# A fused attention and feed-forward kernel on one Trainium2 core: the second attention's output projection as three fp16 passes, with a new step list and new banks

## The chip, the cores and the metric

The kernel runs on one core of one Trainium2 chip. The engines spoken of are TensorE (PE, with PEld for its weight loads), VectorE (DVE), ScalarE (ACT), GpSimd (POOL) and SyncE (SP, which issues the DMAs). The metric is the device time in microseconds (us) of the core; lower is better.

## The reference

For x of 4 x 2048 x 512 in float32, the result of four residual stages:

```
x = x + attn_a(layernorm(x))     # linear attention, 16 heads of 64, prefix sums over tokens
x = x + ffn(layernorm(x))        # int8-rounded matmul with rhs (512 x 512)
x = x + attn_b(layernorm(x))     # gated, decaying state, 16 heads of rank 16
x = x + ffn(layernorm(x))
```

The change lies in the end of `attn_b`, where a state M per head is carried over the tokens:

```
M = M * decay + einsum('bhr,bhd->bhrd', g_t * k_t * scale, v_t)
y = einsum('bhr,bhrd->bhd', q_t, M)
...
out = Y @ out_w.T + out_b
hres = x + out
return (hres - mu) / sqrt(var + 1e-05) * ln_g + ln_b
```

## The kernel before, in words

The 8192 tokens are cut into 64 chunks of 128. For each chunk the work is some 110 named steps; a step belongs to one engine. The table `ORDER` lists every step with a lag. Time is a row of slots; in slot s a step of lag l works on chunk s - l, and each engine walks its own steps in the order of the table. So in one slot PE works on the first attention's projections of chunk s (lag 0), its scores of chunk s - 1, and the second attention of chunk s - 3. Ten slots are written out, then a loop of two slots an iteration runs up to slot 63, then four slots (64 to 67) drain the pipe, each with fewer steps.

Each engine stays in order, so a step that waits holds everything behind it on its engine. `BANK` gives each matmul result one of the 8 PSUM banks; `c.take(unit)` waits until the bank's former user has been read out, `c.read` until it is full, `c.done` until it has been read. `COUNTS` only lists the semaphore values that the loop keeps in registers.

The steps around the change, with their names:
- `yb` (PE) ends y of a chunk in two banks. `y_e` (ACT) copies both to `yT`, which lies in the tile `turn_q`, with the feature in the partition.
- `out` (PE, `out_`) multiplies `yT` by `wout`, both float32: four matmuls of 128x128 by 128x512, each of which the trace shows as two records.
- `out_e` (DVE) adds the bank to `xnb`; `no_st`, `no_rs`, `no_ap`, `no_f` are the layer norm behind it. `nb_ap` (DVE) then writes the next chunk's normalised input into the same `xnb`; `xTb_h`, `xTb_l`, `xTb_t` (ACT, DVE, SP) split it in fp16 halves and transpose them by DMA; `kb`, `gb`, `qb`, `vb` (PE) are its projections.
- All other projections go through `three_pass`: high and low fp16 halves of both operands, three matmuls for one. Their weights are split in the set-up, one after the other, each after its largest absolute value has been found (DVE), spread over the partitions (POOL, `partition_all_reduce`) and turned into a power of two (four small DVE instructions).
- `mm0`, `mm1` (PE) are the two feed-forward matmuls, `mm0_e`, `mm1_e` (DVE) read them out, `mm0_a`, `mm1_a` (POOL) add the residual. `s0`, `so0`, `o0`, `u0` and their twins are the first attention's scores, state products and state update; `qk0` to `qk3` its q and k projections, read out by `qk0_e` to `qk3_e` (DVE).

Of the kernel before, what the change touches and what calls it, by code (L numbers as in the profile page):

```python
# [62 lines left out]
BANK = {"v0": 7, "v1": 1, "qk0": 2, "qk1": 4, "qk2": 6, "qk3": 1, "kt0": 6, "s0a": 2, "s0b": 3, "o0a": 4, "o0b": 5,  # L63
        "u0": 0, "kt1": 0, "s1a": 3, "s1b": 0, "o1a": 6, "o1b": 7, "u1": 1, "wo": 0, "mm0": 0, "qb": 2, "kb": 6,
        "vb": 4, "gb": 7, "qr": 5, "kr": 3, "sb0": 6, "sb1": 7, "sb2": 0, "sb3": 1, "y0": 3, "y1": 5, "ub": 1,
        "out": 7, "mm1": 2}
# [117 lines left out]
def hybrid_kernel(nc, x, Wq, Wk, Wv, Wo, bo, q_w, k_w, v_w, Wqr, Wkr, g_w, g_b, logits, out_w, out_b, ln_g, ln_b,  # L184
                  rhs, tables, keeps, out):
    ctx = ExitStack()
    with ctx:
# [1131 lines left out]
```

## Time and profile before

| | us |
|---|---|
| median of 3 runs | 3245.57 (3244.02 to 3248.7) |
| the profiled execution's own time | 3244.64 |
| its span in the trace | 3242.9 |
| PE busy | 3108.5 (96%) |
| DVE busy | 2179.4 (67%) |
| POOL busy | 1016.1 (31%) |
| ACT busy | 564.6 (17%) |

Busy times are unions over an engine's instructions. A matmul's record is longer than its share of the engine, since the next one starts before it ends; the distance from start to start tells what a matmul costs. L numbers are lines of the kernel before, and a helper's line stands for all its callers: L598 to L600 are the three lines of `three_pass`.

### The profile page before, as it was taken

The numbers are of one execution on the slowest core, as the hardware profiler recorded it, in microseconds if no ns is written. First come the engines' busy times: TensorE is split into PE (matmuls) and PEld (weight loads), VectorE is DVE, ScalarE is ACT, GpSimd is POOL, SyncE is SP. The second block draws the span as 40 slices with busy tenths as digits, with TensorE's granted clock in tenths as the row PEclk, the third lists the DMA queues.
The fourth block names the chain that finished last, engine by engine and source line by source line (L and its number), as shares of the span: only waits on it lengthen the run. The fifth ranks groups of instructions, "written<-read, shape, count | busy, mean of one in ns | idle before, by whom it ended". The sixth has DMA issues, their size and how long they took to land.

```text
span 3242.9 us, 104237 instructions
## 1 busy us (share of the span) xinstructions
PE 3108.5 (96%) x44242; PEld 2368.6 (73%) x44242; DVE 2179.4 (67%) x4675; ACT 564.6 (17%) x1048; POOL 1016.1 (31%) x1371
## 2 busy tenths in 40 slices
PE   1599999999999999999999999999999999999995
PEld 1577777777777777777777777777777777777774
DVE  7566766666766666666676676676676666666664
ACT  2111111111111111111111111111111111111111
POOL 0023333333333333333333333333333333333333
PEclk8799999999999999999999999999999999999998
DMA  4122222222222222222222222222222222222221
GB/s 164 50 43 46 40 47 44 40 47 44 40 47 44 47 42 46 46 43 46 46 40 46 46 40 47 44 40 47 44 40 47 44 45 44 44 46 44 46 39 26
DMA packets 383786, 151.88 MB, mean 47 GB/s; under 512 B 353312, under 2 KB 361632, under 8 KB 383392
## 3 DMA queue, kind: packets, MB, share of 16 engines
q1 hardware_dynamic: 383392, 145.56, 24.3%
q8 instruction: 378, 6.19, 0.8%
q14 instruction: 16, 0.13, 0.0%
HBM read 44.83 MB, written 16.78 MB: 19 GB/s over the span
## 4 chain that ended last, share of the span: by engine, by line
PE 95%; DVE 3%; DMA 1%; issue 1%; ACT 0%; POOL 0%; POOLq 0%; SPq 0%; DVEq 0%; ACTq 0%
PE bank L598 20%; PE bank L600 20%; PE bank L599 20%; PE bank L835 7%; PE bank L659 4%; PE bank L685 4%; PE bank L725 3%; PE bank L565 2%; PE bank L789 2%; PE bank L672 2%; PE bank L768 2%; PE bank L699 2%; PE bank L759 2%; PE bank L812 2%; PE bank L799 1%; DVE absmax L1016 1%
## 5 line engine op out<-in xcount | busy, mean ns | idle before, releaser
L598 PE MATMUL bank<-xaT,wq_hi 128*128 128x128 f16 x2048 | 358.6, 220 | 25.7 <-DMA xaT<-xa_split 25.7
L599 PE MATMUL bank<-xaT,wq_hi 128*128 128x128 f16 x2048 | 357.3, 219 | 0.0
L600 PE MATMUL bank<-xaT,wq_lo 128*128 128x128 f16 x2048 | 357.3, 219 | 0.0
L598 PE MATMUL bank<-xaT,wk_hi 128*128 128x128 f16 x2048 | 356.8, 219 | 0.0
L599 PE MATMUL bank<-xaT,wk_hi 128*128 128x128 f16 x2048 | 356.8, 219 | 0.0
L600 PE MATMUL bank<-xaT,wk_lo 128*128 128x128 f16 x2048 | 356.7, 219 | 0.0
L1105 DVE TENSOR_SCALAR work<-bank,eps_q 128x256 f32<-128x256 f32 x256 | 123.4, 482 | 330.4 <-PE bank L600 330.3
L553 POOL TENSOR_TENSOR xf<-xwb,xf 128x512 f32<-128x512 f32 x64 | 81.8, 1277 | 656.7 <-DVE xf L1185 656.7
L598 PEld LDWEIGHTS bank<-xaT,wq_hi 128*128 128x128 f16 x2048 | 200.6, 98 | 56.3 <-issue 48.6
L835 PE MATMUL bank<-wout,turn_q 128*128 128x512 f32 x512 | 233.8, 599 | 1.9 <-ACT turn_q L942 1.9
L530 POOL TENSOR_TENSOR turn_q<-turn_q,cross_q 128x512 f32<-128x512 f32 x64 | 104.5, 1632 | 334.5 <-DVE cross_q L1209 334.5
L599 PEld LDWEIGHTS bank<-xaT,wq_hi 128*128 128x128 f16 x2048 | 200.8, 98 | 8.3
L600 PEld LDWEIGHTS bank<-xaT,wq_lo 128*128 128x128 f16 x2048 | 200.8, 98 | 0.0
L598 PEld LDWEIGHTS bank<-xaT,wk_hi 128*128 128x128 f16 x2048 | 200.7, 98 | 0.0
L599 PEld LDWEIGHTS bank<-xaT,wk_hi 128*128 128x128 f16 x2048 | 200.6, 98 | 0.0
L600 PEld LDWEIGHTS bank<-xaT,wk_lo 128*128 128x128 f16 x2048 | 200.6, 98 | 0.0
L598 PE MATMUL bank<-wv_hi,xaT 128*128 128x512 f16 x512 | 194.0, 379 | 0.0
L599 PE MATMUL bank<-wv_lo,xaT 128*128 128x512 f16 x512 | 194.0, 379 | 0.0
L600 PE MATMUL bank<-wv_hi,xaT 128*128 128x512 f16 x512 | 194.0, 379 | 0.0
L598 PE MATMUL bank<-wo_hi,work 128*128 128x512 f16 x512 | 194.0, 379 | 0.0
L599 PE MATMUL bank<-wo_lo,work 128*128 128x512 f16 x512 | 194.0, 379 | 0.0
L600 PE MATMUL bank<-wo_hi,work 128*128 128x512 f16 x512 | 194.0, 379 | 0.0
(203 smaller groups left out, 8220.6 us busy)
## 6 DMA issues: line engine op xcount, KB each, us to landing
xin<-in_L_attn_a_x SPq DMA_DIRECT2D x64, 256.0 KB, 2.6
out<-xf SPq DMA_DIRECT2D x64, 256.0 KB, 2.1
table<-in_tables SPq DMA_DIRECT2D x64, 192.5 KB, 2.9
work<-in_L_attn_a_Wq SPq DMA_DIRECT2D x1, 2048.0 KB, 7.8
work<-in_L_attn_a_Wk SPq DMA_DIRECT2D x1, 2048.0 KB, 14.0
work<-in_L_attn_a_Wv SPq DMA_DIRECT2D x1, 2048.0 KB, 7.5
work<-in_L_attn_a_Wo SPq DMA_DIRECT2D x1, 2048.0 KB, 8.4
work<-work SPq DMA_TRANSPOSE x128, 3.6
```

The lines of the kernel that those rows point to most:

```text
L530: pool.tensor_tensor(to[:, :, :, :], to[:, :, :, :], cross[:, :, ::-1, :], ALU.add)\
L553: pool.tensor_tensor(xf1[:, c.par, :], xwb[:, c.par, :], xf1[:, c.par, :], ALU.add)\
L565: last = nc.tensor.transpose(bank[:, i * P:(i + 1) * P], src(i), id_)
L598: nc.tensor.matmul(o, a[0], b[0], start=first, stop=False)
L599: nc.tensor.matmul(o, a[0], b[1], start=False, stop=False)
L600: return nc.tensor.matmul(o, a[1], b[0], start=False, stop=last)
L659: last = nc.tensor.matmul(bank[:, tile(i)], qk[h, 1, 4 * g + i, :], qk[h, 0, 4 * g + i, :], start=True, stop=True)
L672: nc.tensor.matmul(bank[t, i * VA:(i + 1) * VA], qk[h, 0, 4 * g + i, t], state_a[h, 4 * g + i, :], start=i == 0, stop=False, skip_group_ch ...
L685: last = nc.tensor.matmul(bank[t, i * VA:(i + 1) * VA], sc[g][:, p, i, t], va[:, 2 * (4 * g + i) + p, :], start=False, stop=i == 3, skip_g ...
L725: last = nc.tensor.matmul(bank[:, :], xqT[w][:, k, :], rhs_q[:, k, :], start=k == 0, stop=k == KD - 1)
L835: last = nc.tensor.matmul(bank[:, :], yT[:, k, :], wout[:, k, :], start=k == 0, stop=k == KD - 1)
L1105: last = nc.vector.tensor_scalar(qk[:, n, m, :].rearrange("p m t -> p (m t)"), bank[:, 256 * n:256 * n + 256], 0.0, e_[:, :], ALU.max, ALU ...
```

## The change

`wout` becomes a pair of fp16 tiles, scaled by a power of two like the other weights, so the set-up finds a ninth maximum. In each chunk y gets its own scale: `y_m` (DVE) takes the largest absolute value of each partition's row of `yT`, `y_r` (POOL) spreads the largest of all partitions, `y_s` (DVE) makes a power of two and its inverse in four instructions on 128x1, `y_h` (ACT) writes the high half and `y_l` (DVE) the low half into `y_split`, which lies in `cross_q`. `out` is twelve fp16 matmuls, and `out_e` multiplies by the inverse scale as it adds. `ORDER`, `BANK` and `COUNTS` are new throughout; the largest lag stays 4. Of the tables two lines are shown.

```diff
-ORDER = [("nf1_st", 4), ("xTb_h", 3), ("wo1", 2), ("xTb_l", 3), ("qk3", 1), ("s0", 1), ("wo_e", 2), ("kt0", 1),
+         ("y_e", 3), ("y_m", 3), ("aT1_h", 1), ("u1", 1), ("s0", 0), ("aT1_l", 1), ("qk2", 0), ("mm0", 2),
+         ("aT0_t", 1), ("mm1_a", 4), ("ub_e", 3), ("y_r", 3), ("y_s", 3), ("y_h", 3), ("u1_e", 1), ("mm0_e", 2),
+         ("wo0", 1), ("y_l", 3), ("st_o", 4), ("mm0_a", 2), ("qk2_e", 0), ("out", 3), ("nb_st", 2),
...
-        wout = sb("wout", [P, KD, D])
+        wout = (sb("wout_hi", [P, KD, D], F16), sb("wout_lo", [P, KD, D], F16))
...
+        y_split = cross_q[:, :, :, :].rearrange("p j e t -> p (j e t)").bitcast(F16)\
+            .rearrange("p (s k t) -> p s k t", s=2, k=KD)
...
-            for slot in range(8):
+            for slot in range(9):
                 pool.wait_ge(wmax, slot + 1)
...
+            def y_r(c):
+                c.wait(y_reduced, c.count())
+                pool.sem_inc(y_reducing, 1)
+                pool.partition_all_reduce(y_all[:, :], y_max[:, :], P, ABSMAX).then_inc(y_known, 1)
...
             def out_(c):
                 bank, f = c.take("out")
-                c.done("y0")
-                c.done("y1")
+                c.wait(y_halved, c.count())
                 for k in range(KD):
-                    last = nc.tensor.matmul(bank[:, :], yT[:, k, :], wout[:, k, :], start=k == 0, stop=k == KD - 1)
+                    last = three_pass(bank[:, :], (y_split[:, 0, k, :], y_split[:, 1, k, :]), w_part(wout, k, slice(0, D)),
+                                      k == 0, k == KD - 1)
...
+            def y_h(c):
+                c.wait(y_scaled, c.count())
+                c.filled("sb3")
+                nc.scalar.activation(y_split[:, 0, :, :], yT, ACT.Copy, scale=y_scale[:, :]).then_inc(y_hi, 1)
...
-                        if name == "out":
-                            nc.vector.tensor_copy(wout[:, k, :], bank[:, :]).then_inc(e, 1)
-                        else:
...
+            def y_m(c):
+                c.done("y0")
+                c.done("y1")
+                nc.vector.tensor_reduce(y_max[:, :], yT.rearrange("p k t -> p (k t)"), AX_X, ALU.max,
+                                        apply_absolute_value=True).then_inc(y_reduced, 1)
+
+            def y_s(c):
+                c.wait(y_known, c.count())
+                nc.vector.tensor_scalar(y_small[:, :], y_all[:, :], 2.0 ** -80, 2.0 ** -12, ALU.max, ALU.mult)\
+                    .then_inc(y_bounded, 1)
+                c.wait(y_bounded, c.count())
+                nc.vector.tensor_scalar(y_exponent[:, :].bitcast(U32), y_small[:, :].bitcast(U32), 0x7F800000, None,
+                                        ALU.bitwise_and).then_inc(y_power, 1)
+                c.wait(y_power, c.count())
+                nc.vector.tensor_scalar(y_scale[:, :].bitcast(U32), y_exponent[:, :].bitcast(U32), 0x7F800000, None,
+                                        ALU.bitwise_xor).then_inc(y_scaled, 1)
+                nc.vector.tensor_scalar(y_unscale[:, c.par:c.par + 1], y_exponent[:, :], unscale[:, SOUT:SOUT + 1], 0.5,
+                                        ALU.mult, ALU.mult)
+
+            def y_l(c):
+                c.wait(y_scaled, c.count())
+                c.wait(y_hi, c.count())
+                nc.vector.scalar_tensor_tensor(y_split[:, 1, :, :], yT, y_scale[:, :], y_split[:, 0, :, :], ALU.mult,
+                                               ALU.subtract).then_inc(y_halved, 1)
+
             def out_e(c):
                 bank, e = c.read("out")
                 c.wait(xn_bias, c.count())
-                nc.vector.tensor_tensor(xnb[:, :], bank[:, :], xnb[:, :], ALU.add).then_inc(e, 1)
+                nc.vector.scalar_tensor_tensor(xnb[:, :], bank[:, :], y_unscale[:, c.par:c.par + 1], xnb[:, :],
+                                               ALU.mult, ALU.add).then_inc(e, 1)
```

The new list in words, for PE within one slot: `v0 v1 s1 so0 so1 u0 o0 o1 kb gb qb kt1 kr vb kT qr mm1 qk0 sb ys qk1 ub yb u1 s0 qk2 mm0 wo0 out wo1 kt0 qk3`. Before it was: `wo1 qk3 s0 kt0 v0 kt1 v1 kb gb qb s1 so0 so1 o0 u1 u0 o1 kr vb kT qr qk0 sb ys qk1 mm1 mm0 ub yb qk2 out wo0`. `s0`, `kt0` and `qk3` have lag 0 now where they had lag 1.

PE before, in the loop, from the end of `qk2` (the last fp16 rows with `wk`) through `out` (`wout`, four matmuls) to the start of `wo0`:

```order
L598 MATMUL bank<-xaT,wk_hi 128x128
L599 MATMUL bank<-xaT,wk_hi 128x128
L600 MATMUL bank<-xaT,wk_lo 128x128
L123 REGISTER_ALU
L835 MATMUL bank<-wout,turn_q 128x512 x4
L123 REGISTER_ALU
L598 MATMUL bank<-wo_hi,work 128x512
```

PE in the changed kernel, at the end of `wo0` (`wo`) and the start of `out` (`wout`), outside the loop, where the same steps follow each other:

```order
L618 MATMUL bank<-wo_hi,work 128x512
L619 MATMUL bank<-wo_lo,work 128x512
L620 MATMUL bank<-wo_hi,work 128x512
L618 MATMUL bank<-wout_hi,cross_q 128x512
L619 MATMUL bank<-wout_lo,cross_q 128x512
L620 MATMUL bank<-wout_hi,cross_q 128x512
```

`out` stands behind the twelve matmuls of `wo0` now instead of ahead of them, and is made of the same form.

PE in the changed kernel's loop, from `ub` (L845) and `yb` (L832) on, through `u1` (L719) and `s0` (L679) into `qk2`:

```order
L845 MATMUL bank<-vbs,turn_k 32x64 x8
L121 REGISTER_ALU
L832 MATMUL bank<-work,vbs 32x128 x16
L719 MATMUL bank<-va,work 64x65 x8
L679 MATMUL bank<-work 128x128 x8
L618 MATMUL bank<-xaT,wq_hi 128x128
```

`u1` and `s0` have moved between `yb` and `qk2`; behind `qk2` come `mm0`, `wo0` and then `out`.

DVE before, in the loop, from `ub_e` (u_tmp) over `qk1_e`, `qk2_e` and `nb_st` to `out_e` (L1248):

```order
L1242 TENSOR_TENSOR u_tmp<-bank,own_head 128x128
L123 REGISTER_ALU
L1105 TENSOR_SCALAR work<-bank,eps_q 128x256
L1105 TENSOR_SCALAR work<-bank,eps_k 128x256
L1105 TENSOR_SCALAR work<-bank,eps_q 128x256
L1105 TENSOR_SCALAR work<-bank,eps_k 128x256
L1070 BN_STATS stats_b<-xwb 128x6
L1072 COPY carrier<-eps 128x1
L1073 BN_AGGR mean_var_b<-stats_b 128x2
L123 REGISTER_ALU
L1248 TENSOR_TENSOR xnb<-bank,xnb 128x512
```

DVE in the changed kernel's loop, from `y_m` (L1270) over `aT1_l`, `ub_e`, the four instructions of `y_s`, `u1_e` and `mm0_e` (L1207) to `y_l` (L1290):

```order
L1270 TENSOR_REDUCE y_max<-turn_q 128x1
L1115 TENSOR_TENSOR work<-work 128x512
L121 REGISTER_ALU
L1264 TENSOR_TENSOR u_tmp<-bank,own_head 128x128
L1276 TENSOR_SCALAR y_small<-y_all 128x1
L1279 TENSOR_SCALAR y_exponent<-y_small 128x1
L1282 TENSOR_SCALAR y_scale<-y_exponent 128x1
L1284 TENSOR_SCALAR y_unscale<-y_exponent,unscale 128x1
L1161 SCALAR_TENSOR_TENSOR state_a<-state_a,keep_a,bank 128x260
L121 REGISTER_ALU
L1207 SCALAR_TENSOR_TENSOR xf<-bank,row_scale,rs_row 128x512
L1290 SCALAR_TENSOR_TENSOR cross_q<-turn_q,y_scale,cross_q 128x512
```

Six new instructions stand on DVE between `yb` and `out`, and the last of them is queued behind `mm0_e`, which waits for `mm0`.

## Rows read from the trace of the kernel before

**Rows 1.** The page's first part: busy us, share of the span, instructions.

```profile
PE 3108.5 (96%) x44242; PEld 2368.6 (73%) x44242; DVE 2179.4 (67%) x4675; ACT 564.6 (17%) x1048; POOL 1016.1 (31%) x1371
```

**Rows 2.** Stretch from the first to the last full slot: length, busy per engine, clock, DMA.

```profile
117.60:3098.00 2980.40, 2978.94 (x42812) 2273.25 (x42813) 2015.06 (x4368) 519.48 (x985) 959.01 (x1279) 1.00 0.25 44
```

**Rows 3.** Chain that ended last: start us, us, what; two neighbouring slots.

```profile
1573.75 3.49 PE bank L835 x8
1621.90 3.49 PE bank L835 x8
```

**Rows 4.** Timeline of PE, qk2, out, wo: start us, us, engine, line, operation.

```profile
1522.74 0.23 PE L598 MATMUL bank<-xaT,wq_hi 128*128 128x128 f16 x1
...
1525.43 3.65 PE L835 MATMUL bank<-wout,turn_q 128*128 128x512 f32 x8
1528.92 0.38 PE L598 MATMUL bank<-wo_hi,work 128*128 128x512 f16 x1
...
1534.10 0.22 PE L598 MATMUL bank<-xaT,wq_hi 128*128 128x128 f16 x1
```

**Rows 5.** Groups by line: xcount, busy us, mean ns, idle before and its releaser.

```profile
L659 PE MATMUL bank<-work 64*128 64x128 f32 x2048 | 148.7, 285 | 0.0
L1171 DVE TENSOR_REDUCE amax<-xf 128x1 f32<-128x512 f32 x128 | 84.9, 664 | 0.1
L699 PE MATMUL bank<-va,work 128*64 128x65 f32 x2048 | 70.6, 222 | 0.0
L1093 DVE TENSOR_TENSOR cross_k<-xnb,cross_k 128x512 f16<-128x512 f32 x64 | 44.0, 688 | 5.4 <-ACT cross_k L918 0.7
L878 ACT ACTIVATE xa_split<-xna 128x512 f16<-128x512 f32 x64 | 40.3, 630 | 143.2 <-DVE xna L1078 92.1 <-PE bank L600 51.1
```

**Rows 6.** Timeline of all engines around both feed-forward matmuls of one slot.

```profile
1615.99 1.89 PE L725 MATMUL bank<-rhs_q,xqT 128*128 128x512 bf16 x8
1617.05 1.61 DVE L1185 SCALAR_TENSOR_TENSOR xf<-bank,row_scale,rs_row 128x512 f32<-128x512 f32 x2 [1.70 <-PE bank L725]
1617.81 0.43 PE L825 MATMUL bank<-vbs,turn_k 128*32 128x64 f32 x16
1617.88 1.28 POOL L553 TENSOR_TENSOR xf<-xwb,xf 128x512 f32<-128x512 f32 x1 [10.50 <-DVE xf L1185]
```

**Rows 7.** Timelines of POOL and of DVE where two large instructions meet.

```profile
1644.79 1.27 POOL L530 TENSOR_TENSOR turn_k<-turn_k,cross_k 128x512 f32<-128x512 f32 x1 [4.68 <-DVE cross_k L1209]
...
1645.02 1.59 DVE L1093 TENSOR_TENSOR xa_split<-xna,xa_split 128x512 f16<-128x512 f32 x1
```

**Rows 8.** Timelines of DVE, ACT and PE in the set-up, weights bv and out.

```profile
77.28 2.28 DVE L1016 TENSOR_REDUCE absmax<-work 128x1 f32<-128x2048 f32 x1
80.04 0.15 DVE L1019 TENSOR_SCALAR absall<-absall 128x1 f32<-128x1 f32 x1 [0.48 <-POOL absall L490]
...
80.61 2.42 ACT L862 ACTIVATE wbv_hi<-bank,scale 128x512 f16<-128x512 f32 x4 [4.42 <-DVE scale L1022]
...
84.13 1.21 DVE L1016 TENSOR_REDUCE absmax<-work 128x1 f32<-128x1024 f32 x1
...
89.72 3.67 PE L565 MATMUL bank<-ident,work 128*128 128x128 f32 x16 [6.77 <-DMA work<-in_L_attn_b_out_w]
...
94.34 3.62 DVE L1034 TENSOR_REDUCE xwa<-work 128x512 f32<-128x2048 f32 x1
```

**Rows 9.** Timeline of PE in the drain, from slot 65 into slot 66.

```profile
3187.68 1.08 PE L812 MATMUL bank<-work,vbs 128*32 128x128 f32 x32
3189.41 3.67 PE L835 MATMUL bank<-wout,turn_q 128*128 128x512 f32 x8 [0.64 <-ACT turn_q L942]
3202.18 0.26 PE L598 MATMUL bank<-xbT,wbk_hi 128*128 128x128 f16 x1 [9.11 <-DMA xbT<-cross_k]
```

**Rows 10.** Timelines of DVE and PE at the first chunk's first projection.

```profile
115.31 0.69 DVE L1093 TENSOR_TENSOR xa_split<-xna,xa_split 128x512 f16<-128x512 f32 x1 [0.78 <-ACT xa_split L878]
...
119.06 0.27 PE L598 MATMUL bank<-xaT,wq_hi 128*128 128x128 f16 x1 [25.66 <-DMA xaT<-xa_split]
```

More of the change, by code:

```diff
@@ L60 @@
 MAX_LAG = max(LAG.values())
[L63 to L66, printed above, removed]
+BANK = {"v0": 6, "v1": 7, "qk0": 4, "qk1": 3, "qk2": 6, "qk3": 5, "kt0": 7, "s0a": 0, "s0b": 1, "o0a": 2, "o0b": 3,
+        "u0": 7, "kt1": 7, "s1a": 4, "s1b": 0, "o1a": 1, "o1b": 5, "u1": 5, "wo": 4, "mm0": 7, "qb": 4, "kb": 6,
+        "vb": 0, "gb": 0, "qr": 2, "kr": 6, "sb0": 0, "sb1": 1, "sb2": 5, "sb3": 2, "y0": 6, "y1": 7, "ub": 4,
+        "out": 5, "mm1": 3}
 BANKS = 8
@@ L201, in hybrid_kernel @@
         rankk = sb("rankk", [P, 2, 2, P])
-        scale = sb("scale", [P, 8])
-        unscale = sb("unscale", [P, 8])
-        SQ, SK, SV, SO, SBQ, SBK, SBV, SBG = range(8)
+        scale = sb("scale", [P, 9])
+        unscale = sb("unscale", [P, 9])
+        SQ, SK, SV, SO, SBQ, SBK, SBV, SBG, SOUT = range(9)
         eps_q = sb("eps_q", [P, 1])
@@ L295, in hybrid_kernel @@
         squares_i = sb("squares_i", [P, 8, 2])
-        absmax = sb("absmax", [P, 8])
-        absall = sb("absall", [P, 8])
-        exponent = sb("exponent", [P, 8])
+        absmax = sb("absmax", [P, 9])
+        absall = sb("absall", [P, 9])
+        exponent = sb("exponent", [P, 9])
         marks = sb("marks", [P, 16])
+        y_max = sb("y_max", [P, 1])
+        y_all = sb("y_all", [P, 1])
+        y_small = sb("y_small", [P, 1])
+        y_exponent = sb("y_exponent", [P, 1])
+        y_scale = sb("y_scale", [P, 1])
+        y_unscale = sb("y_unscale", [P, 2])
         ps = [ctx.enter_context(nc.psum_tensor(f"bank{i}", [P, 512], F32)) for i in range(BANKS)]
@@ L331, in hybrid_kernel @@
         xn_bias = sem("xn_plus_bias")
+        y_reduced = sem("y_max_of_rows")
+        y_reducing = sem("y_max_begun")
+        y_known = sem("y_max_of_all")
+        y_bounded = sem("y_max_bounded")
+        y_power = sem("y_exponent_ready")
+        y_scaled = sem("y_scale_ready")
+        y_hi = sem("y_hi_done")
+        y_halved = sem("y_split")
         b_added = sem("state_b_added")
@@ L377, in hybrid_kernel @@
         NAT = [("q", Wq, SQ), ("k", Wk, SK), ("v", Wv, SV), ("o", Wo, SO)]
-        TRN = [("bq", q_w, SBQ), ("bk", k_w, SBK), ("bv", v_w, SBV), ("g", g_w, SBG), ("out", out_w, None)]
+        TRN = [("bq", q_w, SBQ), ("bk", k_w, SBK), ("bv", v_w, SBV), ("g", g_w, SBG), ("out", out_w, SOUT)]
         parts = {"q": wa["q"], "k": wa["k"], "v": wa["v"], "o": wo, "bq": wb["q"], "bk": wb["k"], "bv": wb["v"],
-                 "g": wg}
+                 "g": wg, "out": wout}
         TASKS = NAT + TRN + [("rhs", rhs, None)]
@@ L558, in _ @@
                            qb_a=turn("q", turn_q, cross_q), kb_a=turn("k", turn_k, cross_k), gb_k=gb_k, ub_a=ub_a,
-                           mm1_a=mm1_a))
+                           mm1_a=mm1_a, y_r=y_r))
         @block.tensor
@@ L864, in _ @@
                         u += 1
-            act.wait_ge(w_hi, 4 + 4 * KD)
+            act.wait_ge(w_hi, 4 + 5 * KD)
             nc.scalar.activation(amax[:, 0:1], ident[:, 0:1], ACT.Copy).then_inc(ready["act"], 1)
@@ L1045, in _ @@
                         dve.wait_ge(f, u_ // BANKS + 1)
-                        if name == "out":
-                            nc.vector.tensor_copy(wout[:, k, :], bank[:, :]).then_inc(e, 1)
-                        else:
-                            hi += 1
-                            dve.wait_ge(w_hi, hi)
-                            w_hi_, w_lo = parts[name]
-                            nc.vector.scalar_tensor_tensor(w_lo[:, k, :], bank[:, 0:src.shape[0]], scale[:, one],
-                                                           w_hi_[:, k, :], ALU.mult, ALU.subtract).then_inc(e, 1)
+                        hi += 1
+                        dve.wait_ge(w_hi, hi)
+                        w_hi_, w_lo = parts[name]
+                        nc.vector.scalar_tensor_tensor(w_lo[:, k, :], bank[:, 0:src.shape[0]], scale[:, one],
+                                                       w_hi_[:, k, :], ALU.mult, ALU.subtract).then_inc(e, 1)
                         u_ += 1
@@ L1272, in _ @@
                           qb_e=turn_parts("q", turn_q, cross_q), kb_e=turn_parts("k", turn_k, cross_k),
-                          gb_e=gb_e, qr_e=qr_e, kr_e=kr_e, sb_e0=sb_e(0), sb_e1=sb_e(1), ub_e=ub_e, out_e=out_e,
+                          gb_e=gb_e, qr_e=qr_e, kr_e=kr_e, sb_e0=sb_e(0), sb_e1=sb_e(1), ub_e=ub_e, y_m=y_m, y_s=y_s,
+                          y_l=y_l, out_e=out_e,
                           no_st=no_st, no_ap=no_ap, no_f=no_f, nf1_st=nf1_st, nf1_ap=nf1_ap, nf1_q=to_int(1),
```

16 lines of the change are left out of this document (9 added, 7 removed), and 48 rows, old and new, of tables (COUNTS, ORDER).

## The prediction

> **What bounds the kernel now.** I read the busy shares first: PE is busy 96% of the span, DVE 67%, POOL 31%, ACT 17% [rows 1]. Then one window from the first full slot to the last: of 2980.4 us PE is busy 2978.9 at the full clock of 2.4 GHz (granted share 1.00), DVE 2015 [rows 2]. So between set-up and drain PE never stands still, and whatever shortens PE's own stream shortens the kernel one for one, as long as nobody makes PE wait. The chain of waits says the same: it consists of PE, and `out` comes back in it every 1621.90 - 1573.75 = 48.15 us, one slot [rows 3]. Sixty-four chunks make 64 x 48.15 = 3082 of the 3242.9 us; the other 161 are set-up (PE's first projection starts at 119.06 [rows 10]), waits in the drain, and its cold clock.
>
> **The projection itself.** Before, `out` starts at 1525.43 and `wo0` behind it at 1528.92: 3.49 us for four float32 matmuls of 512 columns. `wo0` and `wo1` are 24 fp16 matmuls of the very form that `out` gets, and take 1534.10 - 1528.92 = 5.18 us, 0.216 each [rows 4]. Twelve cost 2.59. That is 0.90 us a chunk less, 64 x 0.90 = 57.6 us.
> PE's other work is the same instructions in another order. By the PE timeline a change from fp16 to float32 steps costs up to 0.09 us at the seam. Before, a slot has five such seams that cost something, now four; I take -0.05 us a slot (between 0 and -0.1), -3.2 us.
>
> **Does PE still find everything ready?** The new work in a slot is a chain between `yb` and `out`: `y_e`, `y_m`, `y_r`, `y_s`, `y_h`, `y_l`. None of these ran in the loop before, so I price each by its nearest row. `y_m` is a maximum over 512 columns, 0.66 (L1171) [rows 5]. `y_r` cost DVE 0.48 of idle time in the set-up (`absall` waiting for POOL), and from there to the start of the ACT instruction that needs the scale is 80.61 - 80.04 = 0.57, which is `y_s` up to its third instruction [rows 8]. `y_h` is L878, 0.63; `y_l` is L1093 on `cross_k`, 0.69 [rows 5]. Sum 3.03, with four hand-overs of some 0.1 us: 3.4 us. `y_e` was there before: where nothing else lay between, `out` started 1.73 us after `yb` did [rows 9]. So the halves are ready 5.1 us after the start of `yb`.
> Behind `yb` (1.08 [rows 9]) PE now has `u1` (70.6 / 128 = 0.55), `s0` (148.7 / 128 = 1.16) [rows 5], `qk2` (1525.43 - 1522.74 = 2.69), `mm0` (half of 1617.81 - 1615.99, 0.91 [rows 6]) and `wo0` (2.59 [rows 4]), so it comes to `out` after 9.0 us. The chain by itself has 3.9 us to spare.
> But `y_l` is queued behind `mm0_e` on DVE. `mm0` ends 6.4 us after the start of `yb`; DVE starts to read a feed-forward bank about 0.2 us after its four matmuls (1617.05 against 1615.99 + 0.86, as `mm1` is half of the eight) and takes 0.7 to 0.8 [rows 6]. So `y_l` starts at 7.3 and ends at 8.0, 0.9 us ahead of `out`. Cover for that is `wo0`; without it `out` would wait 1.7 us a slot.
> The other close places I found by laying PE's new list out in time with the old distances: `s0` needs `qk1_e` (about 0.7 to spare), `qk2` needs the bank of `y0` (0.9), `u0` needs `v0_e` (0.9), `o1` needs `s1_e` (1.1), `yb` needs the four masks of `sb` (0.9). None is negative. DVE gets 0.66 + 0.6 + 0.69, about 2 us, more a slot, and was busy for 68% of it [rows 2]; ACT 0.63, POOL 0.36. No engine but PE becomes full. I count zero a slot; the bounds are 0 and 0.4 (below).
>
> A rule speaks against `y_l`. In the trace `xa_split`, which has two inputs in SBUF as `y_l` has, took 1.59 us where POOL's addition of 1.27 had begun 0.23 before it, while the same form took 0.69 on `cross_k` [rows 5, 7]: it ended 0.55 after POOL's. The Trainium skill, page "SBUF — State Buffer", section "SBUF: two separate sides", says why: VectorE and GpSimd share a port pair as an exclusive lock, the first to start keeps it, the other is blocked fully; by that rule, the trace agrees. Now `mm0_a` on POOL and `y_l` on DVE are both let go by `mm0_e`. In the trace POOL starts 0.83 us after DVE's read-out began [rows 6], and DVE's next instruction after 0.7 to 0.75, so `y_l` should win by about 0.1. If it loses, it ends 0.83 + 1.24 + 0.55 = 2.6 us after the start of `mm0_e`, where PE comes to `out` after 2.59 - 0.2 = 2.4; with the hand-over that is up to 0.4 us of waiting a slot.
>
> **Set-up.** `out`'s weights land at 89.7 (PE begins to transpose them), and the next weight maximum could start there. One weight from its maximum to the next one's start is 84.13 - 77.28 = 6.85 us, so DVE would be free for `rhs` at 96.6 instead of 94.34 [rows 8]: +2.2 us (0 to 3).
>
> **Filling the pipe.** Slots 0 to 2 lack the lag-3 steps, so PE comes early. `s0` with lag 0 stands right behind `qk1` and waits for `qk1_e`, some 1.0 us in slot 0, 0.5 in slots 1 and 2. `qk0` of slots 1 and 2 now comes about 10.3 us into its slot; its transposed input needs `s1_e` first (7.7 us into the slot), then the low half and the DMA, 119.06 - 115.31 = 3.75 [rows 10]: 11.4, so 1.1 us twice. Together +4.2 (0 to 8). Before, PE went through here without a wait.
>
> **Draining it.** In slots 64, 65 and 66 the fillers of lag 0 and 1 are gone, so the 3.4 us of the y chain lie open; and there each chunk's `kb` waits for the `out` of the chunk before, since both use `xnb`: 3202.18 - 3189.41 = 12.8 us from one to the other, 9.11 of it idle [rows 9]. In slot 64 `wo0` and `mm0` still fill, but this only moves work ahead of the same chain. So three chunks pay in full: 3 x 3.4 = +10.2 us (7 to 13).
>
> **Sum.** -57.6 - 3.2 + 2.2 + 4.2 + 10.2 = -44.2. The profiled execution took 3244.64 by its own time, 1.74 around its span; it becomes 3200.4. It was 0.9 under the median of the runs, so I forecast 3201 us for the median.
>
> **Rivals.**
> - Dense, and the ends for free: filling and draining hidden by something I overlook, set-up too. 3201 - 16.6 = 3184. For it: DVE is idle for a third of each slot. Against it: the drain is a pure chain, its waits stand in the trace.
> - Thin margins tear: `y_l` loses the port to `mm0_a`, or `s0` or `u0` find their reader late, 0.4 us in each of some 60 slots: +24, 3225. For it: a margin of 0.1 us in the port race, margins under 1 us elsewhere. Against it: the old list has waits as close and shows none.
> - The other side: `y_r` is dear inside the loop. It is the only kind of instruction that POOL had in the set-up alone, and POOL's spans are rough. The chain has 3.3 us to spare until `out` (2.4 until `mm0_e` ends, 0.9 behind it), and the gain is 44 / 60 = 0.7 a slot; so the kernel gets slower once `y_r` costs over 4.0 us more than its 0.48. At 6 us it would be 3201 + 60 x 2.2 + 3 x 5.5 = 3350. For it: a call of 128x512 is longer than one of 128x1 and the loop has other POOL work around it. Against it: eight calls in the set-up, and DVE's wait confirms the 0.48 from outside.
> - Three passes come out still cheaper. The trace has 0.216 us for each of the 512-column fp16 matmuls, in a dense stream with all its weight loads [rows 4]. If such a stream could go at 0.13, `out` would take 1.6 and 64 x 1.0 more would be gained: about 3137. The Trainium skill, page "TensorE: Matmul & The Clock Gate", section "Back-to-back issue gap", gives about 131 ns as the sustained distance at 512 columns; the trace contradicts it.
>
> **How the numbers follow.** Dense slots with ends that cost something 0.66, ends for free 0.12, thin margins 0.13, dear `y_r` 0.07, cheaper passes 0.01, anything else 0.01. The time is that of the first, 3201. Its own range is 3193 to 3210 (set-up, filling, draining and seams at their bounds). The range to hold the time 8 times in 10 reaches to the second and third: 3182 to 3230. A measurement of this kernel tells 0.2% (6.5 us) from no change. The first three cases and the fifth are all faster by more than that: 0.91. Within 0.2% only by a stall that happens to be 0.7 us a slot: 0.02. Slower: 0.07.
>
> **What would show it.** Right: a slot of 47.2 us in the chain; PE busy without a gap from the first full slot to the last; twelve records of 0.38 us in `out`, 0.216 apart; PE idle ahead of `out` only in slots 64 to 66, some 3 to 4 us released by DVE's `y_l`; POOL's reduction near 0.36; `y_l` near 0.7. Wrong: PE idle ahead of `out` in the loop, with `y_l` at 1.3 or more (the port), or with POOL's reduction as releaser; PE idle ahead of `s0`, `u0`, `o1` or `qk2` in each slot; a slot that isn't 0.9 us shorter although PE never waits.

## The result, and the profile after

The changed kernel takes 3525.43 us (median of 4 runs, 3519.92 to 3529.04) against 3245.68 of the kernel before in the same comparison: a ratio of 1.0861, 95% interval 1.0843 to 1.0878. It is slower by 280 us where 44 us of gain were forecast. The profiled execution took 3523.69, its span is 3521.9.

The page's first part, as in [rows 1]:

```profile
PE 3120.6 (89%) x44370; PEld 2358.5 (67%) x44498; DVE 2264.2 (64%) x5064; ACT 612.5 (17%) x1116; POOL 1052.2 (30%) x1436
```

One window inside the run of full slots (columns as in [rows 2]):

```profile
237.00:3400.00 3163.00, 2934.63 (x42050) 2216.80 (x42171) 2072.44 (x4688) 555.33 (x1036) 997.53 (x1340) 0.98 0.21 41
```

PE, busy throughout before, is idle for 228 of these 3163 us, and its granted clock is no longer full. From `out` to `out` a slot now takes 51.95 us in the mean (52 slots) instead of 48.15. The groups by line name the wait (xcount, busy us, mean ns, then the idle time before them and its releaser):

```profile
L569 POOL PARTITION_ALL_REDUCE y_all<-y_max x64 | 26.2, 409 | 870.5 <-issue 870.5
L618 PE MATMUL bank<-wout_hi,cross_q 128*128 128x512 f16 x256 | 115.0, 449 | 170.6 <-DVE cross_q L1290 170.6
L1092 DVE BATCH_NORM_STATS2 stats_b<-xwb 128x6 f32<-128x512 f32 x64 | 44.5, 695 | 325.4 <-POOL xwb L531 325.4
L1276 DVE TENSOR_SCALAR y_small<-y_all 128x1 f32<-128x1 f32 x64 | 9.8, 154 | 373.7 <-POOL y_all L569 373.7
L531 POOL TENSOR_TENSOR xwb<-xwa,xf 128x512 f32<-128x512 f32 x64 | 80.4, 1256 | 456.2 <-issue 442.4
```

The reduction itself takes 0.41 us, as hoped. But before it GpSimd is idle for 870.5 / 64 = 13.6 us by "issue", that is, by nothing the profile shows (part of it GpSimd would be idle anyway, until `y_m` is done), and its next ordinary instruction, the addition of `mm0_a`, waits another 442.4 / 63 = 7.0. DVE's `y_s` loses 5.8 us a slot to the first, `nb_st` 5.1 to the second.

The list of one line's instructions says what stands there. `y_r` (L569) and the helper of GpSimd's additions (L531):

```profile
L569 POOLq MODIFY_POOL_CONFIG  x128: 11/11/11, 231.4 to 3490.2; - x128
L569 POOL PARTITION_ALL_REDUCE y_all<-y_max x64: 408/409/412, 237.4 to 3496.1; - x64
```

```profile
L531 POOLq MODIFY_POOL_CONFIG  x126: 82/83/83, 237.8 to 3451.4; - x126
```

(The three numbers are the least, median and largest duration in ns, then come the first and the last start in us.) Two reconfigurations go ahead of each of the 64 reductions, and two at `mm0_a` behind 63 of them. From the reconfiguration to the reduction it is 237.4 - 231.4 = 6.0 us in the first chunk and 3496.1 - 3490.2 = 5.9 in the last. I call what happens in this time a load of code; the trace shows only the idle time behind the reconfiguration. In the kernel before there was a pair for the reductions too, once:

```profile
L490 POOLq MODIFY_POOL_CONFIG  x2: 11/11/11, 3.6 to 3.6; - x2
```

The first of its eight reductions began at 13.4 us, after a wait for the maximum of the first weights, so the load that goes with it lay under that wait.

One slot in time. DVE and then GpSimd (start us, us, instruction, idle before it and releaser):

```profile
1526.63 0.69 DVE L1270 TENSOR_REDUCE y_max<-turn_q 128x1 f32<-128x512 f32 x1 [0.86 <-ACT turn_q L962]
...
1534.02 0.15 DVE L1276 TENSOR_SCALAR y_small<-y_all 128x1 f32<-128x1 f32 x1 [5.90 <-POOL y_all L569]
...
1534.98 0.74 DVE L1207 SCALAR_TENSOR_TENSOR xf<-bank,row_scale,rs_row 128x512 f32<-128x512 f32 x1
1535.64 0.74 DVE L1290 SCALAR_TENSOR_TENSOR cross_q<-turn_q,y_scale,cross_q 128x512 f16<-128x512 f32 x1
...
1542.21 0.69 DVE L1092 BATCH_NORM_STATS2 stats_b<-xwb 128x6 f32<-128x512 f32 x1 [5.05 <-POOL xwb L531]
...
1543.10 0.72 DVE L1296 SCALAR_TENSOR_TENSOR xnb<-bank,y_unscale,xnb 128x512 f32<-128x512 f32 x1
```

```profile
1533.58 0.41 POOL L569 PARTITION_ALL_REDUCE y_all<-y_max  x1 [13.75 <-issue]
1540.93 1.25 POOL L531 TENSOR_TENSOR xwb<-xwa,xf 128x512 f32<-128x512 f32 x1 [6.95 <-issue]
```

The chain of waits crosses the same place (start us, us, what):

```profile
1527.78 5.80 issue
1533.58 0.42 POOL y_all L569
```

`y_m` is done at 1527.3. Some 0.4 us go to handing over and to the reconfigurations, the wait by "issue" behind them takes 5.80, and at 1533.58 the reduction begins. Then the ordinary code comes back, 6.95 us, with `mm0_a` behind it, `nb_st` behind that on DVE, and `out_e` behind `nb_st`.

PE in the same slot:

```profile
1533.66 0.38 PE L620 MATMUL bank<-wo_hi,work 128*128 128x512 f16 x1
1536.53 0.38 PE L618 MATMUL bank<-wout_hi,cross_q 128*128 128x512 f16 x1 [2.49 <-DVE cross_q L1290]
...
1537.61 0.63 PE L620 MATMUL bank<-wout_hi,cross_q 128*128 128x512 f16 x1
...
1540.59 0.59 PE L618 MATMUL bank<-wo_hi,work 128*128 128x512 f16 x1
```

`out` waits 2.49 us. Its matmuls start 0.216 apart at first and 0.43 apart from 1537.61, so PE has fallen from 2.4 to 1.2 GHz behind the idle time: the twelve take 4.06 us instead of 2.59. The granted clock of the stretch from 1537.90 to 1541.00 is 0.50:

```profile
1537.90:1541.00 3.10, 3.10 (x8) 1.06 (x7) 0.00 (x0) 0.00 (x0) 0.07 (x1) 0.50 0.00 0
```

This happens in 20 of the 52 slots, not in each. In the other 32 `out` takes its 2.59 us, and `qk3` waits 1.7 us for `out_e` instead, since `out_e` now frees `out`'s bank late (63.1 us in 43 slots, the whole run taken together). The two kinds of slot are equally long, 51.8 and 52.0 us: what ends a slot is `out_e`, at the end of GpSimd's way back.

### The profile page after: what moved, and what is told of

Same layout as the page of the kernel before. It is cut to its first block, busy times and chain, and to the rows that moved or that the text cites. A ratio compares the mean times of both kernels' runs of the same rounds, so it can differ in the third digit from the quotient of the medians.

```text
span 3521.9 us, 104781 instructions
## 1 busy us (share of the span) xinstructions
PE 3120.6 (89%) x44370; PEld 2358.5 (67%) x44498; DVE 2264.2 (64%) x5064; ACT 612.5 (17%) x1116; POOL 1052.2 (30%) x1436
## 3 DMA queue, kind: packets, MB, share of 16 engines
q8 instruction: 379, 6.21, 0.7%
## 4 chain that ended last, share of the span: by engine, by line
PE 65%; issue 21%; DVE 8%; POOL 3%; ACT 1%; DMA 1%; POOLq 0%; ACTq 0%; DVEq 0%; SPq 0%
PE bank L618 16%; PE bank L620 15%; PE bank L619 15%; PE bank L705 3%; PE bank L679 2%; PE bank L809 2%; PE bank L692 2%; POOL xwb L531 2%; PE bank L788 2%; PE bank L779 2%; PE bank L745 1%; PE bank L585 1%; PE bank L832 1%; DVE y_max L1270 1%; PE bank L719 1%
## 5 line engine op out<-in xcount | busy, mean ns | idle before, releaser
L618 PE MATMUL bank<-xaT,wq_hi 128*128 128x128 f16 x2048 | 361.6, 221 | 94.9 <-DVE xnb L1296 63.1
L618 PE MATMUL bank<-xaT,wk_hi 128*128 128x128 f16 x2048 | 361.3, 221 | 0.0
L619 PE MATMUL bank<-xaT,wk_hi 128*128 128x128 f16 x2048 | 361.1, 221 | 0.0
L569 POOL PARTITION_ALL_REDUCE y_all<-y_max x64 | 26.2, 409 | 870.5 <-issue 870.5
L618 PE MATMUL bank<-wout_hi,cross_q 128*128 128x512 f16 x256 | 115.0, 449 | 170.6 <-DVE cross_q L1290 170.6
L1092 DVE BATCH_NORM_STATS2 stats_b<-xwb 128x6 f32<-128x512 f32 x64 | 44.5, 695 | 325.4 <-POOL xwb L531 325.4
L1276 DVE TENSOR_SCALAR y_small<-y_all 128x1 f32<-128x1 f32 x64 | 9.8, 154 | 373.7 <-POOL y_all L569 373.7
L531 POOL TENSOR_TENSOR xwb<-xwa,xf 128x512 f32<-128x512 f32 x64 | 80.4, 1256 | 456.2 <-issue 442.4
L620 PE MATMUL bank<-wv_hi,xaT 128*128 128x512 f16 x512 | 195.1, 381 | 6.2 <-issue 5.7
L618 PE MATMUL bank<-xbT,wbk_hi 128*128 128x128 f16 x1024 | 179.1, 222 | 19.5 <-DMA xbT<-cross_k 19.5
L618 PE MATMUL bank<-wo_hi,work 128*128 128x512 f16 x512 | 195.8, 382 | 0.6 <-DVE u_tmp L1264 0.6
```

Of the source, the lines that this page charges most:

```text
L531: pool.tensor_tensor(xwb[:, c.par, :], xwa[:, :], xf0[:, :], ALU.add).then_inc(x2_ready, 1)
L618: nc.tensor.matmul(o, a[0], b[0], start=first, stop=False)
L619: nc.tensor.matmul(o, a[0], b[1], start=False, stop=False)
L620: return nc.tensor.matmul(o, a[1], b[0], start=False, stop=last)
L1092: nc.vector.bn_stats(stats[n][:, :], src).then_inc(stat[n], 1)
```

## The experiments

The first four ran beside the same runs of the kernel before (median 3244.96), the next four beside 3244.99, the last three beside 3244.97 and 3245.37.

**Without the reduction.** `y_r` is taken out, and `y_s` makes its scale from each partition's own maximum.

```diff
-                           mm1_a=mm1_a, y_r=y_r))
+                           mm1_a=mm1_a))
...
-                c.wait(y_known, c.count())
-                nc.vector.tensor_scalar(y_small[:, :], y_all[:, :], 2.0 ** -80, 2.0 ** -12, ALU.max, ALU.mult)\
+                c.wait(y_reduced, c.count())
+                nc.vector.tensor_scalar(y_small[:, :], y_max[:, :], 2.0 ** -80, 2.0 ** -12, ALU.max, ALU.mult)\
```

> The changed kernel without y_r: y_s makes each partition's scale from its own maximum, so the spread over the partitions is left out and the output projection mixes scales. Theory A (GpSimd reloads its code before partition_all_reduce and again before its next ordinary instruction, 5.8 and 6.95 us, and all else is as forecast): no reload, PE dense, a slot of 47.2 us, 3200 us (3190 to 3212). Theory B (the new list or banks stall PE by themselves, the reload is only part): the slot stays over 48 us, above 3250.

Measured: 3229.13 us, ratio 0.9951 (0.9934 to 0.9968), above the range of A. So the reduction alone makes the loss: 3525 - 3229 = 296 us. But 28 us of the forecast gain are missing here too. Every other slot is 47.18 us, just as forecast; those in which the loop turns are longer, and the waits of PE show time by "issue" in `v0`, the first step of the new list:

```profile
PE bank L620 <- issue: 9.6, 23, 0.8
```

**The reduction runs, nobody waits for it.** Does the wait of `y_s` make the loss, or that GpSimd is away? (`y_m` now waits for the reduction of the chunk before, which reads `y_max` too; by its idle time this costs it nothing.)

```diff
+                c.wait(y_known, c.count(1))
                 nc.vector.tensor_reduce(y_max[:, :], yT.rearrange("p k t -> p (k t)"), AX_X, ALU.max,
...
-                c.wait(y_known, c.count())
-                nc.vector.tensor_scalar(y_small[:, :], y_all[:, :], 2.0 ** -80, 2.0 ** -12, ALU.max, ALU.mult)\
+                c.wait(y_reduced, c.count())
+                nc.vector.tensor_scalar(y_small[:, :], y_max[:, :], 2.0 ** -80, 2.0 ** -12, ALU.max, ALU.mult)\
```

> y_r still runs in every slot but y_s doesn't wait for it (each partition's own maximum makes its scale, as in the run without it). Theory A: out no longer waits for its halves, but GpSimd's way back stays: mm0_a comes 13 us after y_m, nb_st on VectorE waits for it, out_e behind nb_st, qk3 for out_e's bank: some 4 us of PE idle ahead of qk3 each slot, about 3450 (3380 to 3500). Theory C (only the reload ahead of the reduction matters, since that is the one in the chain to out): about 3210.

Measured: 3652.89 us, ratio 1.126 (1.1242 to 1.1279), slower even than the changed kernel. With `y_s` free, `out` no longer waits; `qk3` does, for `out_e` (PE's waits: in all, times, longest):

```profile
PE bank L618 <- DVE xnb L1297: 264.5, 61, 5.1
```

The way back alone, through `mm0_a`, `nb_st` and `out_e`, holds PE 4.3 us in nearly every slot, where I expected some 4. The rest is the clock, which the forecast left out: behind this one long wait it falls in each of the 52 slots, for 5.8 us a slot in the mean, where it was 1.6 in the changed kernel. The granted clock of a window of full slots is 0.95 against 0.98, and the same 44370 matmuls keep PE busy for 3188.4 us against 3120.6. A slot takes 53.99 us, and my 3450 was too low by 200.

**The code is brought in early.** The changed kernel with one more reduction, behind `mm1_a`, where GpSimd has nothing to do; its result is unused. The scale is still that of the chunk's maximum.

```diff
+                pool.partition_all_reduce(y_dup[:, :], absmax[:, 0:1], P, ABSMAX)
```

> A second partition_all_reduce of an unchanging tile behind mm1_a, early in the slot, so that the reduction's code is there when y_r comes; output as in the changed kernel. Theory A: y_r runs within 0.5 us of y_m, the reload of ordinary code behind it is over before mm0_e ends, a slot near 47.3, about 3206 (3195 to 3225). Theory D (a reduction of fresh data in the loop is slow whatever code is loaded, or each one reloads): the loop has twice the reductions, 3525 or more.

Measured: 3262.8 us, ratio 1.0058 (1.0042 to 1.0075): one more instruction a slot saves 263 us. It is still 38 us above the range of A. The reduction that loads the code waits by "issue", the one that DVE waits for hardly does:

```profile
L570 POOL PARTITION_ALL_REDUCE y_all<-y_max x64 | 37.9, 592 | 98.0 <-DVE y_max L1272 79.8 <-issue 18.2
L576 POOL PARTITION_ALL_REDUCE y_dup<-absmax x64 | 26.2, 409 | 382.4 <-issue 382.4
```

In the loop the slots are 47.18 again, but for the turns, which make the mean 47.58. Outside the loop, where fewer fillers stand, the loads lie open: PE's first projection starts at 128.85 us against 121.42 in the changed kernel, and the last two distances from `out` to `out` are 44.07 and 41.44 us, against 36.31 and 34.32 without the reduction.

**List and banks alone.** The kernel before, float32 projection and all, with the new list and banks.

```diff
-ORDER = [("nf1_st", 4), ("xTb_h", 3), ("wo1", 2), ("xTb_l", 3), ("qk3", 1), ("s0", 1), ("wo_e", 2), ("kt0", 1),
+ORDER = [("v0", 1), ("wo_e", 2), ("ld_x", 0), ("no_f", 4), ("s0_e", 1), ("nb_ap", 3), ("qk3_e", 1), 
...
-        "out": 7, "mm1": 2}
+        "out": 5, "mm1": 3}
```

> The kernel before with the new list (without the five y steps) and the new banks; float32 projection as before. Theory A: PE dense in a slot of 48.1 us, 4 us more in filling the pipe: 3245 to 3252. Theory B (the list stalls): above 3270.

Measured: 3250.22 us, ratio 1.0014 (1.0004 to 1.0024). Slots of 48.02, 0.13 less than before, and more at the ends. No gap at the turn of the loop. So the new order by itself makes none of the loss in the loop.

**A constant scale.** `y_m`, `y_r` and `y_s` are gone. The largest |Y| of the reference for these inputs is 30263; times 2^-6 it is 473, well inside fp16.

```diff
-                nc.scalar.activation(y_split[:, 0, :, :], yT, ACT.Copy, scale=y_scale[:, :]).then_inc(y_hi, 1)
+                nc.scalar.activation(y_split[:, 0, :, :], yT, ACT.Copy, scale=2.0 ** -6).then_inc(y_hi, 1)
...
-                nc.vector.scalar_tensor_tensor(xnb[:, :], bank[:, :], y_unscale[:, c.par:c.par + 1], xnb[:, :],
+                nc.vector.scalar_tensor_tensor(xnb[:, :], bank[:, :], y_unscale[:, 0:1], xnb[:, :],
```

> Leaves out the maximum, the reduction and the scale chain of each chunk: y_m, y_r and y_s are gone, y_h and y_l use the constant 2^-6, and out_e its inverse. A (the reload of GpSimd's code is the whole of the loss, and what is left of the y chain is short): 3229 of the run without the reduction, less 1.1 us (y_m and y_s) in each of the three draining slots, so 3225 (3219 to 3231); slots of 47.2, with the same gap in v at each turn of the loop. B (the changed kernel also pays for the two passes of halves, y_h and y_l, in the loop): slots over 47.6 all through, with PE idle ahead of out, and 3250 or more.

Measured: 3226.43 us, ratio 0.9942 (0.9925 to 0.9959). The gap in `v0` stays, 12 us in all, and `out` doesn't wait in the loop: with `y_m`, `y_r` and `y_s` the whole loss is gone.

**PE's code moved by 64 instructions.**

```diff
+            for _ in range(64):
+                pe.wait_ge(s_pool, 1)
             pe.wait_ge(s_pool, 8)
```

> The kernel with the constant scale, and 64 waits that are met at once at the head of PE's program, so that its loop begins 64 instructions later in PE's code; nothing else differs. A (the gap of 0.2 to 1.2 us in v at each turn of the loop comes from where the loop's first instruction lies in the pieces in which code is fetched): the gap leaves the 26th matmul behind the branch and is gone or much smaller, 12 to 18 us less than its twin without the waits, so about 3210. B (the gap comes of what v waits for or of the data it reads): the gap stands at the same matmul, and the time is within 3 us of the twin.

Measured: 3262.81 us, ratio 1.0049 (1.0032 to 1.0066). The gap did move, from the 26th to the 15th matmul after the branch, so that it hangs on where the loop lies and not on data; but it grew, where I expected it to go. 36 us from 64 waits that cost nothing by themselves:

```profile
PE bank L620 <- issue: 46.0, 26, 2.6
```

The 26 and 15 count matmuls in time, and the first 14 of them still belong to `qk3`, issued ahead of the branch. In the order of the code the gap stood ahead of the twelfth matmul of `v0` and now stands ahead of its first, at the branch itself. The branch's own records say the same. Without the 64 waits, and then with them:

```profile
L384 PEldq COMPARE_BRANCH  x27: 88/357/394, 625.1 to 3094.9; - x27
L384 PEldq COMPARE_BRANCH  x27: 88/2272/3337, 624.6 to 3136.6; - x27
```

**The reduction in the kernel before.** One reduction behind `xhb` in each slot of the old list, result unused.

```diff
                 pool.tensor_tensor(xnb[:, :], xnb[:, :], outb_row[:, :], ALU.add).then_inc(xn_bias, 1)
+                pool.partition_all_reduce(y_dup[:, :], absmax[:, 0:1], P, ABSMAX)
```

> The kernel before, with its own list and banks, and one more partition_all_reduce of 128x1 on GpSimd behind xhb in each slot; nobody waits for its result. A (each change between the reduction and ordinary instructions loads code, about 6 us one way and 7 us the other, in any list): two reconfigurations a slot, GpSimd idle by issue some 6 to 13 us ahead of the reduction and 7 us ahead of the next addition; GpSimd was busy for only a third of a slot, but the addition behind it is late by up to 10 us, so PE waits in each slot: 3300 to 3650. B (the price belongs to the new list, where the reduction stands beside mm0_a): no such idle time, 3245 to 3252.

Measured: 3258.67 us, ratio 1.0041 (1.0027 to 1.0055). Both loads are there, 378.1 / 64 = 5.9 and 452.2 / 63 = 7.2 us, in another list and with no `y_m`:

```profile
L523 POOL PARTITION_ALL_REDUCE y_dup<-absmax x64 | 26.2, 409 | 378.1 <-issue 378.1
L555 POOL TENSOR_TENSOR xf<-xwb,xf 128x512 f32<-128x512 f32 x64 | 80.3, 1255 | 459.7 <-issue 452.2 <-DVE xf L1187 7.5
```

So A is right on the load and wrong on the time: the slot stays at 48.15, because GpSimd was idle ahead of that addition anyway (10.50 us in [rows 6]). Only the drain grew. The price per slot is the same 13 us; what it costs hangs on who is waiting.

**Two reductions in a row.** A second one right ahead of that of `y_r`.

```diff
                 pool.sem_inc(y_reducing, 1)
+                pool.partition_all_reduce(y_dup[:, :], y_max[:, :], P, ABSMAX)
                 pool.partition_all_reduce(y_all[:, :], y_max[:, :], P, ABSMAX).then_inc(y_known, 1)
```

> The changed kernel with a second reduction right ahead of the one in y_r, of the same size, its result unused. A (the price is that of changing kinds, and a reduction behind a reduction costs its 0.4 us): 64 times 0.4 to 0.5 more than the changed kernel, 3551 (3535 to 3570). B (each call of a reduction in the loop costs about 6 us): 64 times 6 more, 3850 to 3950.

Measured: 3551.48 us, ratio 1.0941 (1.0923 to 1.0959), 3551 forecast. The first waits as before, the second not at all:

```profile
L571 POOL PARTITION_ALL_REDUCE y_all<-y_max x64 | 27.4, 427 | 0.0
L570 POOL PARTITION_ALL_REDUCE y_dup<-y_max x64 | 26.2, 409 | 869.7 <-issue 869.7
```

The price is that of changing from one kind of instruction to the other, not of a call.

**The old list with three passes and the constant scale.** `y_h` behind `y_e`, `y_l` behind `ub_e`, otherwise list and banks of before.

```diff
-         ("mm0_e", 2), ("mm1_a", 4), ("yb", 3), ("mm0_a", 2), ("ld_t", 2), ("y_e", 3), ("qk2", 0), ("aT0_t", 1),
-         ("ub_e", 3), ("out", 3), ("qk1_e", 0), ("wo0", 1), ("qk2_e", 0), ("aT1_t", 1), ("nb_st", 2),
+         ("mm0_e", 2), ("mm1_a", 4), ("yb", 3), ("mm0_a", 2), ("ld_t", 2), ("y_e", 3), ("y_h", 3), ("qk2", 0), ("aT0_t", 1),
+         ("ub_e", 3), ("y_l", 3), ("out", 3), ("qk1_e", 0), ("wo0", 1), ("qk2_e", 0), ("aT1_t", 1), ("nb_st", 2),
```

> The list and banks of the kernel before, with the three-pass projection and the constant scale: y_h stands behind y_e, y_l behind ub_e, out stays between qk2 and wo0. A (the new list only costs at the ends: 12 us in the first slots and 12 to 14 us at the turns of the loop, which now lie behind short matmuls): slots of 48.15 less 0.90 = 47.25, no gap at the turns, ends as in the kernel before, but for 2 to 4 us more in the set-up and about 1.5 us of y_h and y_l in each of three draining slots: 3244.6 - 57.6 + 3 + 4.5 = 3195 (3190 to 3202). C (the new list is needed, since the halves come too late for out in the old one: 3.3 us of chain against 3.77 of cover): PE idle ahead of out in each slot, released by y_l, 0.3 to 1 us; 3215 to 3260.

Measured: 3199.72 us, ratio 0.9864 (0.9847 to 0.9882). Slots of 47.25, exactly 0.90 under 48.15, and none waits for `out`'s halves: three waits in the whole run, 7.6 us, all in the drain. The new list is not needed for the three passes with a constant scale; with `y_m`, `y_r` and `y_s` in the chain nobody tried the old one.

**160 waits instead of 64** (`range(160)`), in the kernel with the new list and the constant scale.

> As the kernel with 64 waits at the head of PE's program, with 160. 64 moved the gap from the 26th matmul behind the branch to the 15th and made it 1.6 to 2.1 us. A (the gap sits where a piece of code of 256 instructions or less ends): 160 puts the end of the piece at another place, far enough behind the branch that the next piece is there in time, and the gap is gone: 3226 less 14, 3212 (3208 to 3217). D (the piece is of 64 or 32 instructions, so that 160 is a place like 64 or like 0): a gap at the 15th or the 26th matmul again, 3226 to 3263.

Measured: 3202.17 us, ratio 0.9868 (0.9851 to 0.9886), 24 us less than without the waits, 61 less than with 64, and 6 below the range of A. The branch takes 0.45 us in the median. PE is busy without a break (window of full slots, columns as in [rows 2]), and a slot takes 47.17:

```profile
618.00:3060.00 2442.00, 2442.00 (x35930) 1880.53 (x35929) 1720.75 (x3732) 456.36 (x880) 819.30 (x1091) 1.00 0.22 45
```

**Early reduction and 160 waits together**, in the changed kernel, nothing left out.

> The changed kernel, whole, with a reduction of its own behind mm1_a whose result is unused (it brings GpSimd's code in while nobody waits), and 160 waits at the head of PE's program. A (the two losses, reload and gap at the turn, are apart and add up): 3263 of the kernel with the early reduction alone, less the 24 us that the 160 waits gave the kernel with the constant scale, 3239 (3232 to 3246), loop slots of 47.2 with no gap, and the rest of the distance to 3202 in the slots outside the loop, where the reload lies open. B (with the reduction in the loop something else waits too): slots over 47.3, more than 3246.

Measured: 3239.15 us, ratio 0.9981 (0.9972 to 0.999), 3239 forecast: the two losses are separate and add up. Five gaps in `v0` are left in the window, 1.6 us in all, and a slot takes 47.24 in the mean (47.17 in the median, 48.02 at most). With both mended the change is at last 6 us faster than the kernel before.

The version to keep, for data whose y is bounded, is one of the two at 3200 to 3202 us, faster than both kernels; they lie less than 0.1% apart, and the runs don't tell them apart.

## Why the prediction was wrong

**The step that failed is the price of `y_r`.** It was read in the set-up, 0.48 us of DVE waiting [rows 8], and taken into the loop. There it costs DVE 5.90, and GpSimd another 7.0 on the way back, which the sum put at nothing. What [rows 8] show is a reduction that follows a reduction; a reduction among additions first waits for a reconfiguration of GpSimd, in the changed kernel, in the kernel before with one reduction put in, and not when two stand in a row. I gave that case 0.07, on the right ground (the only kind of GpSimd instruction that the set-up alone had), and thought the eight calls evidence against it. They were eight calls with one load between them. "DVE's wait confirms the 0.48 from outside" was true and of no help. The Trainium skill, page "GPSIMD Engine Reference", section "Instruction dispatch", says that the first call to a freshly loaded kernel pays an extra load of about 6 us behind a `MODIFY_POOL_CONFIG`. The 5.80 and 5.9 us here agree, and the prediction had overlooked it.

**The rival's price was short too.** "Dear `y_r`" at 6 us gave 3350. Its first part held: `out` waits 2.4 us in the mean of the 52 slots, with 2.2 forecast. What it left out are two things that come after. The way back to ordinary instructions takes GpSimd another 7.0 us, delays `mm0_a`, `nb_st` and `out_e`, and makes `qk3` wait 1.1 us a slot in the mean. And PE's clock sometimes falls behind its idle time: `out` is 1.55 us longer in 20 of the 52 slots, 0.6 in the mean. With 0.2 of smaller waits this is 4.3 of the 51.95 - 47.18 = 4.8 us by which a slot is over a dense one; another 0.2 stands in five slots whose clock fell behind `qk3`'s wait, 53.9 us long each, and 0.3 I can't place. The parts are not independent. The run whose `out` doesn't wait was no shorter, and where `out` is slow `qk3` waits 0.1 us: the way back holds the slot, and taking away the wait ahead of `out` alone would gain nothing. In [rows 2] the clock was 1.00, and I priced waits as if it stayed there.

**The projection: right.** Twelve matmuls take 2.59 us; with PE's other work unchanged (old list) the slot fell by 0.90, to 47.25. With the new list it is 47.17 to 47.18, and 47.2 was forecast. The seams gave 0.13 (48.02 against 48.15), in which I had 0.05 with bounds of 0 and 0.1.

**The rest of the y chain: right.** `y_m` 0.69 (0.66 forecast), `y_s` up to `y_scale` from 1534.02 to ACT's start at 1534.58, 0.56 (0.57), `y_h` 0.72 (0.63), `y_l` 0.74 (0.69).

**The thin margins held.** With the reduction's code loaded early and the gap nearly gone, the whole chain runs in slots of 47.24 in the mean. The race of `y_l` with `mm0_a` is not seen in that run or in the changed kernel, where `mm0_a` comes some 3 and 5 us later. It is in the run without the reduction: there `mm0_a` begins 0.16 us behind `y_l` in each slot that has both (some 0.1 was forecast), `y_l` keeps its 740 to 750 ns in all 64 chunks, and the addition, 1.26 us in the changed kernel, takes 1.70. In the old list with three passes `y_l` begins behind `mm0_a` and takes up to 1.50 us; that list has room for it. So the forecast had the race right, and the margin is as thin as it said.

**Set-up, filling, draining: the sum was short.** PE's first projection began at 121.42 in the changed kernel; 119.06 + 2.2 = 121.3 was forecast. (It was 122.1 without the reduction and 123.0 to 123.8 with the constant scale, and I can't say why; so the 0.1 us of agreement is in part luck.) Taking from the span the time up to there and the 60 distances between the `out`s of the 61 full slots, the ends are 234.4 us before, 247.3 with list and banks alone, 249.0 with 160 waits, and 239.6 with the old list. So the new list costs 12.9 us where 4.2 were down for it, before any y chain. Nearly all of it lies in the filling: from PE's first projection to the first `out` it is 118.3 us against 106.2. PE waits there for `xaT` and in `s0`, but I have not decomposed the rest. The drain was sized better. Behind the `out` of the last full slot the run without the reduction takes 141.6 us, list and banks alone 129.0. Of these 12.6 us, 6.0 are one more gap by "issue" and its clock (47.8 us to the next `out`, against 41.8 with 160 waits), and four shorter `out`s hide 3.6. So the y chain without `y_r` costs some 10 us there, where 10.2 - 3 x 0.48 = 8.8 follow from the prediction.

**Not foreseen: the gap at the turn of the loop.** In the run without the reduction it made 14 of the missing 28 us (a mean slot of 47.46 against a median of 47.19, over 52 slots); another 8.7 are the ends of the new list. It was nobody's rival. I had weighed what each step waits for, and not what it costs PE to begin the loop anew behind another step. The runs with 64 and 160 waits show that it depends on where the loop's first instruction lies in PE's code. Code comes in pieces of 16 KB by the page's count (6.21 MB in 379 packets). In three kernels the stall stands in the branch's own record (a record of the sequencer, which runs ahead of PE's matmuls), 2.27 us in the median with 64 waits, 3.49 in the kernel before and 3.71 in the kernel before with a reduction in each slot, against 0.36 to 0.47 in the others. Before:

```profile
L370 PEldq COMPARE_BRANCH  x27: 87/3487/3965, 611.6 to 3115.7; - x27
```

So the kernel before had this stall, longer than the one with 64 waits, and PE never stood still: in the turn at 1574.6 us ten matmuls of `out` and `wo0`, 0.216 us and more from start to start, begin while the branch waits. In the new list 14 of `qk3`, 0.056 apart, cover 0.8 us of it. It is the short matmuls at the loop's end that lay a stall at the branch open. Why one position brings a stall at the branch, another eleven matmuls behind it and a third none stays open; that the old list with three passes has none (0.45 us) is luck of position as far as the runs show. The Trainium skill, page "Runtime: NRT & Kernel Launch", section "Instruction fetch mechanics", states blocks of 256 instructions and a stall at a taken branch whose target isn't at hand; that the gap moves with the position, and the branch's 2.27 us, agree.

**A slip in the chances.** The four cases that are faster add up to 0.66 + 0.12 + 0.13 + 0.01 = 0.92, not 0.91; nothing hangs on it.

## What to carry to other kernels

Price an instruction by what ran on its engine just before it, not only by its own rows: a `partition_all_reduce` among ordinary GpSimd instructions costs about 6 us there and 7 us back, and a set-up that runs eight in a row hides both. Then ask which wait comes next: with the one ahead of `out` gone, the one ahead of `qk3` took its place. Look for reconfigurations among the queue's own instructions; if the reduction must stay in the loop, put a dummy one where GpSimd is idle and nobody waits. And when a loop's steps are rotated, look at the first matmuls behind its turn: 64 waits ahead of it cost 36 us and 160 were worth 24. Long matmuls ahead of the turn cover a stall there, short ones don't.

## What the runs showed of the hardware

- Reconfiguring GpSimd: 5.8 to 6.0 us from an addition to a reduction (5.80 in the slot shown, 382.4 / 64 and 378.1 / 64 where nothing else was waited for) and 7.0 to 7.2 back (442.4 / 63 and 452.2 / 63), in the changed kernel and in the kernel before alike; a reduction behind a reduction has 0.0 us of idle time.
- Behind 2.2 to 2.8 us of idle time PE's matmuls of 512 columns started 0.43 us apart, from the sixth on in the slot shown, in 20 of 52 slots, and stayed at 0.216 in the other 32. Behind 3.7 to 5.1 us of idle time the clock fell in each of 52.
- A GpSimd addition of 128x512 that began 0.16 us behind a DVE instruction with two inputs in SBUF took 1.70 us instead of 1.26, and the DVE instruction its usual 0.74.
- PE's branch at the loop's turn takes 0.36 us, 2.27 with 64 more instructions ahead of the loop and 0.45 with 160; the same PE loop takes 3226, 3263 and 3202 us in all.
